# A pairwise graph-attention kernel on one core: who forms the differences, who takes their signs away, and how many difference tiles there are

## What is computed

```
h = relu(layernorm(x))                           # 64 x 128 x 128
D = abs(h[:, :, None, :] - h[:, None, :, :])
p = einsum('bijc,oc->bijo', D, W1) + b1          # 64 outputs per pair
m, v = mean and variance of p over b, i, j
p = leaky((p - m) / sqrt(v + EPS) * g1 + be1)
s = where(adj > 0, p @ W2 + b2, NEG)
A = softmax(s);  y = (A @ h) @ Wg.T + bg;  y = leaky(batchnorm(y))
x = x + concatenate([h, y]) @ Wt.T + bt
x = x + second_layer(relu(layernorm(x)), adj)    # attention of the usual kind
```

## Time and profile before

| what | value |
|---|---|
| median of three runs | 1194.98 us (1191.22 to 1197.27) |
| the profiled execution: time, span | 1195.55 us, 1193.8 us |
| pass one | up to about 667 us |
| pass two and the attention | to about 1035 us |
| busy over the whole span | PE 89%, DVE 89%, ACT 83%, POOL 45% |
| granted TensorE clock, mean | 0.964 |

### The profile page before, as it was taken

One profiled execution on the slowest core, in us unless ns is written; L12 is line 12 of the kernel. 1 busy time (PEld: TensorE's weight loads), 2 busy tenths in 40 slices (PEclk: granted clock), 3 DMA queues, 4 the chain that ended last, 5 costly groups with the idle time before them and its releaser, 6 DMA issues.

```text
span 1193.8 us, 17535 instructions
## 1 busy us (share of the span) xinstructions
PE 1065.4 (89%) x6376; PEld 465.2 (39%) x6376; DVE 1058.0 (89%) x1418; ACT 994.3 (83%) x1238; POOL 541.6 (45%) x251
## 2 busy tenths in 40 slices
PE   3889999999999999999999589899999999547886
PEld 1323333333333333333333212233333333437886
DVE  6899999999999999999999788999999998445776
ACT  3879999999999999999999599898989887017787
POOL 5466667666666666666566001111111111136551
PEclk9989999999999999999999799999999999668998
DMA  5324343434343434333434799999999996403322
GB/s 164 131 117 176 142 177 141 177 142 177 142 177 151 167 142 177 156 162 156 177 160 177 275 339 366 360 349 339 348 354 339 361 335 232 119 26 90 90 80 72
DMA packets 118005, 237.52 MB, mean 199 GB/s; under 512 B 17568, under 2 KB 65952, under 8 KB 117920
## 3 DMA queue, kind: packets, MB, share of 16 engines
q1 hardware_dynamic: 116336, 235.70, 54.2%
q10 hardware_dynamic: 1584, 0.69, 0.2%
HBM read 126.52 MB, written 109.84 MB: 198 GB/s over the span
## 4 chain that ended last, share of the span: by engine, by line
PE 44%; DVE 33%; ACT 10%; issue 6%; POOL 3%; DMA 3%; SPq 0%; DVEq 0%; ACTq 0%; POOLq 0%
PE psum L696 18%; DVE store L272 12%; PE psum L706 10%; PE psum L710 7%; DVE plain_st L967 4%; ACT store L598 4%; DVE store L1045 2%; ACT store L544 2%; PE psum L809 2%; DMA early<-score_rows 1%; POOL small L474 1%; PE psum L766 1%; PE psum L668 1%; PE psum L686 1%; DVE ln_st L904 1%
## 5 line engine op out<-in xcount | busy, mean ns | idle before, releaser
L696 PE MATMUL psum<-store,w1tt_sb 128*64 128x512 f32 x1792 | 426.0, 605 | 36.1 <-ACT store L544 19.2
L272 POOL TENSOR_TENSOR store<-h_ext 128x2048 f32<-128x2048 f32 (+1 forms) x96 | 386.5, 4029 | 141.0 <-PE psum L696 137.1
L272 DVE TENSOR_TENSOR store<-psum,h_ext 128x2048 f32<-128x2048 f32 x160 | 363.8, 2274 | 0.0
L544 ACT ACTIVATE store<-store 128x2048 f32<-128x2048 f32 x160 | 305.1, 1930 | 15.1 <-DVE store L272 10.2
L696 PEld LDWEIGHTS psum<-store,w1tt_sb 128*64 128x64 f32 x1792 | 121.7, 137 | 276.1 <-issue 223.4
L598 ACT ACTIVATE store<-store,st 128x1024 f32<-128x1024 f32 x192 | 226.3, 1245 | 1.6 <-DVE st L1033 1.4
L706 PE MATMUL psum<-store,w_twice 128*64 128x512 f32 x768 | 201.6, 603 | 3.9 <-DVE early L932 3.5
L967 DVE BATCH_NORM_STATS2 plain_st<-store 128x6 f32<-128x512 f32 x256 | 160.5, 677 | 0.6 <-ACT store L556 0.6
L710 PE MATMUL psum<-early 128*64 128x512 bf16 x1152 | 158.1, 381 | 0.0
L272 DVE TENSOR_TENSOR store<-h_ext 128x2048 f32<-128x2048 f32 x64 | 137.4, 2147 | 2.6 <-PE psum L696 2.5
L766 PE MATMUL psum<-store,w_rows 128*32 128x512 f32 x1024 | 131.8, 606 | 5.4 <-ACT store L598 5.4
(11 more groups left out here) (153 smaller groups left out, 1151.4 us busy)
## 6 DMA issues: line engine op xcount, KB each, us to landing
kept_products<-store SPq DMA_DIRECT2D x192, 512.0 KB, 2.7
store<-kept_products SPq DMA_DIRECT2D x192, 512.0 KB, 7.4
early<-score_skew SPq DMA_DIRECT2D x16, 384.0 KB, 6.8
early<-adj SPq DMA_DIRECT2D x16, 256.0 KB, 8.0
store<-x SPq DMA_DIRECT2D x16, 256.0 KB, 3.8
store<-adj_t SPq DMA_DIRECT2D x16, 256.0 KB, 3.2
out<-store SPq DMA_DIRECT2D x16, 256.0 KB, 2.7
score_rows<-early SPq DMA_DIRECT2D x64, 32.0 KB, 3.3
```

The lines of the kernel that those rows point to most:

```text
L272: return engine.tensor_tensor(t[:, :, 0:steps, :], nodes.unsqueeze(2).broadcast_to([C, 2, steps, N]), windows(h_ext[:, 2 * c, :], STEP * m ...
L544: nc.scalar.activation(t, t, ACT.Abs).then_inc(abs_ready, 1)
L696: last = nc.tensor.matmul(t[MID * g:MID * g + MID, b, :], w1tt_sb[:, 0:MID], diff[slot][:, g, b * BANK:b * BANK + BANK], start=True, stop= ...
```

## The change

In pass one:

- `MAXED` goes from m = 0, 3, 6 to m = 0, 4. `POOLED` goes from m = 1, 4, 7 to m = 1, 3, 5, 7. VectorE now makes the tiles of m = 0, 2, 4, 6.
- The tile of m = 2 gets its absolute value on VectorE: `clear` clears the sign bits with one `tensor_scalar` on the tile, after the counts of that step; TensorE waits for a semaphore of its own, `cleared`. ScalarE takes the absolute values of m = 1, 3, 5, 6, 7 (before: 1, 2, 4, 5, 7), five as before.
- `SLOTS` goes from 5 to 7 difference tiles. The room comes from the nodes' parts, of which four quads are held in turn instead of all sixteen (`YRING`), and from tiles of pass two that now lie over `kept`. ScalarE waits for the last stores of two `kept` tiles ahead of pass two.
- The ring of pass two has 12 tiles instead of 10; its first ten loads wait for the last use of difference tiles, the others for `kept` tiles. On SP's queue the attention's DMAs stand 12 steps behind the loads instead of 10.

```
-MAXED = (0, 3, 6)
-POOLED = (1, 4, 7)
+MAXED = (0, 4)
+POOLED = (1, 3, 5, 7)
+CLEARED = (2,)
...
-SLOTS = 5
+SLOTS = 7
+YRING = 4
...
-DIFFED = tuple(m for m in range(PER) if m not in MAXED)
+ABS_ON_ACT = tuple(m for m in range(PER) if m not in MAXED + CLEARED)
...
-        loaded = [tiles(8 + 2 * s, 2) for s in range(10)]
+        loaded = [tiles(8 + 2 * s, 2) for s in range(12)]
...
-            return y_parts[:, 2 * u:2 * u + 2, n, :]
+            return y_parts[:, 2 * (u % YRING):2 * (u % YRING) + 2, n, :]
...
-                elif k < 6:
+                elif k < 10:
                     sp.wait_ge(prod_ready, last_use(2 + k // 2) + 1)
...
             act.wait_ge(pass2_ready, 1)
+            for z in (2, 3):
+                act.wait_ge(kept_stored[z], NKEPT // ZRING * 16)
...
-                    pe.wait_ge(abs_ready, before(DIFFED, n) + 1)
+                    if n % PER in CLEARED:
+                        pe.wait_ge(cleared, before(CLEARED, n) + 1)
+                    else:
+                        pe.wait_ge(abs_ready, before(ABS_ON_ACT, n) + 1)
...
+            def clear(n):
+                bits = diff[n % SLOTS].bitcast(I32)
+                dve.wait_ge(diff_ready, before(BY_DVE, n) + 1)
+                nc.vector.tensor_scalar(bits, bits, 0x7FFFFFFF, None, ALU.bitwise_and).then_inc(cleared, 1)
...
+                if n < CHUNKS and n % PER in CLEARED:
+                    clear(n)
```

More of the change, by code:

```diff
@@ L121, in two_layers @@
         h_ext = sb("h_ext", [C, B, EXT])
-        store = sb("store", [128, 32, BANK])
+        store = sb("store", [128, 36, BANK])
         def tiles(at, n):
@@ L128, in two_layers @@
         diff = [tiles(4 * s, 4).rearrange("p (g x) -> p g x", g=2) for s in range(SLOTS)]
-        kept = [tiles(20 + 2 * s, 2) for s in range(ZRING)]
-        loaded = [tiles(8 + 2 * s, 2) for s in range(10)]
+        kept = [tiles(28 + 2 * s, 2) for s in range(ZRING)]
+        loaded = [tiles(8 + 2 * s, 2) for s in range(12)]
         LRING = len(loaded)
-        leaky = [tiles(28 + 2 * s, 2) for s in range(2)]
-        early = sb("early", [128, 8704])
-        y_parts = early[:, 0:6144].bitcast(BF16).rearrange("p (c s x) -> p c s x", c=COUPLES, s=PARTS)
-        pair_nodes = early[:, 6144:8704].bitcast(BF16).rearrange("p (m x) -> p m x", x=WIDE)
+        leaky = [tiles(32 + 2 * s, 2) for s in range(2)]
+        early = sb("early", [128, 5120])
+        y_parts = early[:, 0:1536].bitcast(BF16).rearrange("p (c s x) -> p c s x", c=2 * YRING, s=PARTS)
+        pair_nodes = early[:, 1536:1536 + 512 * len(MAXED)].bitcast(BF16).rearrange("p (m x) -> p m x", x=WIDE)
         def late(at, n):
@@ L186, in two_layers @@
             "placed", "pool_diff", "copies_counted", "stat_squares"))
+        cleared = sem("cleared")
         diff_ready, abs_ready, prod_ready, taken, counted, kept_ready, shift_mm, shift_ready = (sem(n) for n in (
@@ L326, in load_kept @@
                     sp.wait_ge(scored, last // 2 + 1)
-                elif k < 6:
+                elif k < 10:
                     sp.wait_ge(prod_ready, last_use(2 + k // 2) + 1)
                 else:
-                    z = k - 6
+                    z = k - 10
                     sp.wait_ge(kept_stored[z], NKEPT // ZRING * 16)
@@ L570, in _ @@
                         do(u)
-                if n < CHUNKS and n % PER in DIFFED:
+                if n < CHUNKS and n % PER in ABS_ON_ACT:
                     absolute(n)
@@ L710, in products_by_max @@
                             last = nc.tensor.matmul(t[MID * g:MID * g + MID, b, :],
-                                                    y_parts[:, c, s, MID * g:MID * g + MID],
+                                                    y_parts[:, c % (2 * YRING), s, MID * g:MID * g + MID],
                                                     pair_nodes[:, k, b * BANK:b * BANK + BANK],
```

## The result

The changed kernel takes 1214.97 us (median; 1212.71 to 1217.72), the one before 1195.08 in the same measurement. The ratio is 1.0167, with a 95% interval of 1.0143 to 1.0192: slower by 20 us. The prediction said slower, 1208, with a range of 1196 to 1230. The profiled execution took 1217.72 us.

The account below looks back on a forecast made before the run. The prediction took TensorE as nearly full, with ScalarE handing it a few inputs just in time. 0.85 us more in each of 15 quads gave 12.8, other terms zero: 1195.55 + 12.8 = 1208 us, range 1196 to 1230.

Parts of the forecast that it names:

- The loop: Pass one, ScalarE's and TensorE's queues through chunk 3's absolute value: quad 40.14 us against 39.29, 12.8 us more in all.
- The clear: VectorE's sign clearing for chunks 2 and 10 waits for POOL but ends in time: zero, up to 4.8 us a quad otherwise.
- rival 2: In pass one VectorE's clear falls behind POOL's next subtraction: 1280 us if always, 1244 with half; chance 0.15.
- The tiles: Seven difference tiles in pass one let POOL start earlier, which it needed; no wait for it on the path.
- The start: Fewer node patterns on POOL before pass one's first chunks: 0, within 1 us either way.
- Pass two: Two more tiles in its load ring give 0, at best 3 us gained, at worst 6 us lost.
- Rival 1: In pass one load decides, so faster: quad at ScalarE's 36.99 us, 1161 us, half the gain 1178; chance 0.12.

## Why the prediction was right, and where it wasn't

**The loop** was right, in place and in size. It was walked to 40.14 us from rows of before alone; the trace has 40.17, and the stations between agree within 0.03, so this isn't luck. ScalarE's busy time (36.99), TensorE's stop for chunk 3 (forecast: over 2 us, found 2.22) and ScalarE's wait for the transposes (about 2, found 1.81) came as described. The loads were nearly right (TensorE 36.34 for 35.7, VectorE 35.74 for 35.3, POOL 32.86 for 33.4). Moving single steps shortened quads as the same walk said: 39.43 for 39.4, 38.90 for 38.9, 38.15 for 38.0.

**The step that was missing** is the clock. The sum took chunk 3 at 1.86 us after the stop, from a row with a stop of 0.98 us. In eight of the 14 quads it took 2.35 to 3.56, since the granted clock had fallen, and 11.2 us of the profiled execution lie there. Filling the stop gave 8 us back in the medians; with a stop of 1.5 us no steady quad had a slow chunk 3.

**The clear** was set at zero on the path. It isn't on the loop, but it costs 10 us in all. The statement that VectorE's room covers its waits held in steady quads only; leaving the clear out shortened the first four quads and the stretch ahead of them. That a clear meets a POOL subtraction is common and mostly free: 15 of 32 took 2.0 to 3.1 us, as the prediction expected, and TensorE waited for two of them, 7.1 us in all, both early, where VectorE came late. That is the cause that rival 2 names, VectorE's lateness, in two places and not in every quad; its other half, a clear behind the subtraction of m = 7, didn't happen at either.

**The tiles** were said to be needed by POOL and off the path. Off the steady loop is right: the old split gains nothing from seven, and with this split two quads had 40.16 and 40.17 on five tiles. That POOL needs them is likely (8 us by the medians) and not clear of noise.

**The start** was set at zero within 1 us. Without the accident it gained 0.9; but POOL's earlier first difference, taken as harmless, is what made the accident possible.

**Pass two** was set at zero: the difference is under 1 us.

**Rival 1** (load decides) fell as it stood. But it was right that load allows more: with the order mended, the same split runs in quads of 37.9 us.

So 1208 was the loop alone. Above it stand the slow chunk 3 and the late clears: 18.2 us of excess in the quads, against 10.5 that the kernel before has too and that the forecast had left standing, 7.7; the start (without the accident) and pass two take 1.8 off. That makes 1195.1 + 12.5 + 7.7 - 1.8 = 1213.5; the last 1.5 us to the median I can't place. This sum is of the profiled execution less its accident, and the median may have another share of the slow chunk 3 and the late clears. The forecast fell within 7 us because its one large term was right; the two effects that it set at nothing, half clock and late clears, make up most of the rest.

## What to carry to other kernels

When work moves between engines whose queues are in order, compare loads last. Walk one round along the queues and the waits, with spacings from the trace, and check the walk on the kernel before; here it gave the length of a steady quad within 0.2 us four times and was 0.4 short once. A short operation that another engine's input now stands behind (`normalise`, 1.55 us) can cost more than the work saved, and moving it by a step is free. And look at how long TensorE stands still, not only how much in all: a stop can also slow what comes after it.

## What the runs showed of the hardware

- A stop of TensorE of 2.2 us was followed by a stretch at a granted clock of 0.54 in every second quad; with four more matmuls put into the same stop, and in steady quads where it was 1.5 or 1.1 us long, chunk 3 took 1.87 us. Length alone doesn't decide: stops of 2.05 and 2.01 us elsewhere were followed by two chunks in 3.59 us.
- A clear (`tensor_scalar` on 128x2048 in SBUF) takes 1.2 us alone and up to 4.42 us (4.13 in the rows above) when POOL is in a subtraction, whose end it waits for; the doubling of 64 elements a partition 0.20 and 4.06 us.
- VectorE's differences with one input in PSUM took 2.27 us whether POOL was busy for 45% or 57% of the span.
